# Audio tower on one Trainium2 core: the shared network's last product in eleven matmuls, and two reorderings beside it

## What is computed

```python
q, k, v = split(x, 3, axis=1)                       # each (128, 125, 512)
h = v @ softmax(q.T @ k / sqrt(125)).T              # per batch: 512 x 512 scores
n = layernorm(h)
h = h + attention(n; Wq, Wk, Wv, Wo)                # 8 heads, 2 kv heads, rope, tanh softcap 50
n = layernorm(h)
shared = (silu(n @ sw1) * (n @ sw3)) @ sw2          # sw2: 448 x 512
routed = top-2 of 8 experts (softmax(n @ gate_w) + bias), each the same network with w1, w3, w2
out = h + shared + routed
```

## Time and profile before

| | us |
|---|---|
| three runs | 6224.49, 6225.23, 6228.56 |
| median | 6225.23 |
| the profiled execution, device time | 6225.23 |
| its span, first to last instruction | 6223.5 |

### The profile page before, as it was taken

How to read it: one execution, slowest core, us unless ns; L and a number is a source line. 1 busy time by engine, 2 the same in 40 slices (tenths; PEclk the granted TensorE clock), 3 DMA queues, 4 the chain that set the end, 5 groups by cost and what they waited for, 6 DMA issues and landing times. The chain is left out here.

```text
span 6223.5 us, 108360 instructions
## 1 busy us (share of the span) xinstructions
PE 6034.7 (97%) x32968; PEld 5134.6 (83%) x32968; DVE 3931.3 (63%) x9812; ACT 2617.3 (42%) x4904; POOL 2608.1 (42%) x1865
## 2 busy tenths in 40 slices
PE   5999999999999999999999996999999999999999
PEld 4888888888888888888888885888888888888888
DVE  4777777777777777777777774444444444444444
ACT  3444444444444444444444442333333333333332
POOL 1333333333333333333333333555555655555554
PEclk8999999999999999999999998999999999999999
DMA  2111111111111111111111113555555555555541
GB/s 69 48 44 44 47 41 47 44 44 47 42 49 41 46 45 43 48 41 48 43 44 47 42 40 102 138 143 141 143 144 143 132 140 145 137 143 144 143 105 48
DMA packets 273407, 495.61 MB, mean 80 GB/s; under 512 B 39444, under 2 KB 112148, under 8 KB 273236
## 3 DMA queue, kind: packets, MB, share of 16 engines
q1 hardware_dynamic: 202452, 363.37, 19.6%
q0 software_dynamic: 70912, 131.71, 10.4%
HBM read 370.13 MB, written 140.28 MB: 82 GB/s over the span
## 5 line engine op out<-in xcount | busy, mean ns | idle before, releaser
L1325 POOL DMA_INDIRECT out_dram<-res,goal x280 | 519.4, 1855 | 929.9 <-DVE res L1261 446.1
L619 ACT ACTIVATE e<-ps,shift 128x512 f32<-128x512 f32 x512 | 347.9, 684 | 671.1 <-DVE shift L718 635.3
L1193 ACT ACTIVATE rT_hi<-ps 128x512 fp32r<-128x512 f32 x280 | 167.9, 600 | 1040.2 <-PE ps L1129 1040.2
L1119 PE MATMUL ps<-e_hi,rT_hi 128*128 128x448 f32 x2240 | 596.9, 388 | 5.2 <-ACT rT_hi L1193 5.2
L1303 POOL TENSOR_TENSOR e_lo<-raw,e_hi 128x1792 fp32r<-128x1792 f32 x140 | 568.6, 4062 | 9.8 <-ACT e_hi L1188 6.5
L1261 DVE COPY res<-ps 128x512 f32<-128x512 f32 x280 | 193.7, 692 | 594.8 <-PE ps L1119 579.8
L1119 PE MATMUL ps<-e_lo,rT_hi 128*128 128x448 f32 x2240 | 550.8, 367 | 0.0
L1119 PE MATMUL ps<-e_hi,rT_lo 128*128 128x448 f32 x2240 | 549.4, 367 | 0.0
L904 POOL TENSOR_SCALAR ve<-ag 125x1 f32<-125x1 f32 x256 | 57.1, 223 | 1124.7 <-DVE ag L734 1087.0
L1119 PEld LDWEIGHTS ps<-e_hi,rT_lo 128*128 128x128 f32 x2240 | 421.2, 188 | 37.8
L1119 PEld LDWEIGHTS ps<-e_lo,rT_hi 128*128 128x128 f32 x2240 | 421.2, 188 | 37.3
(11 more groups left out here) (203 smaller groups left out, 15377.0 us busy)
## 6 DMA issues: line engine op xcount, KB each, us to landing
raw<-in_L_ffn_w SPq DMA_DIRECT2D x210, 896.0 KB, 5.6
X<-in_x SPq DMA_DIRECT2D x128, 750.0 KB
normed_rows<-y SPq DMA_DIRECT2D x128, 250.0 KB
out_dram<-h SPq DMA_DIRECT2D x128, 250.0 KB
rows<-normed_rows,entries POOLq DMA_INDIRECT x280, 4.8
out_dram<-res,goal POOLq DMA_INDIRECT x280
routed_entries<-entry,slot POOLq DMA_INDIRECT x256
raw<-in_L_ffn_sw SPq DMA_DIRECT2D x3, 896.0 KB
```

What stands on the lines that cost most here:

```text
L619: nc.scalar.activation(e[:, i, :], ps[:, (i + 1) % 2, :], ACT.Exp, scale=QS, bias=shift[:, i:i + 1], accum_out=total[:, i:i + 1]).then_inc ...
L1119: ins = nc.tensor.matmul(dst, lhs[a][:rows_, k, :], rhs[b][:rows_, k, 0:width], start=(k == 0 and i == 0), stop=(k == KC - 1 and i == 2))
L1325: nc.gpsimd.indirect_dma_start(out, bass.IndirectOffsetOnAxis(ap=goal[group[1] % 2][:, i:i + 1], axis=0), res[i % 2][:], None, bounds_chec ...
```

## The change

`sw2` has 448 = 3 x 128 + 64 rows. It is now held as three pieces 128 deep and a fourth whose lower and upper 64 partitions both hold the last 64 rows (two loads into `raw_2[:, 3, :]`). The hidden activation is cut alike (`turn_inner`: three transposes of 128 columns and one of 64). Of its last piece the high part stands in partitions 0 to 63 of `hT[0]`, and the low part, which was in `hT[1]`, in partitions 64 to 127 of the same. One matmul with `w2s` high then does high x high and low x high at once; the other, with `w2s` low (zero in the upper half), does high x low. So three pieces take three matmuls each and the last takes two: 11.

Since `down_part(3, 0)` now needs the low part too, the downs are put elsewhere: four ahead of `scores(2)` (two ahead of the X transposes, two behind, the second of these waits for `hT_lo`), none between `scores(2)` and `scores(3)`, four behind the xn transposes. Three stay at the step's end. ScalarE makes hT_hi, and VectorE the low part, in two instructions each.

On ScalarE xT_hi now comes ahead of vT_high. On GpSimd vT_low now comes behind the second `rstd` and the two scatters.

```diff
-        w2s = resident("w2s", [HW, HC, D])
+        w2s = resident("w2s", [P, HC, D])
+        TAIL = HID - 3 * P
...
-                    load(raw_2[:, :, :], sw2.rearrange("(k p) h -> p k h", p=HW))
+                    load(raw_2[:, 0:3, :], sw2[0:3 * P, :].rearrange("(k p) h -> p k h", p=P))
+                    for q in range(2):
+                        load(raw_2[q * TAIL:(q + 1) * TAIL, 3, :], sw2[3 * P:HID, :])
...
+                    nc.vector.memset(w2s[1][TAIL:P, 3, :].bitcast(F32), 0.0)
+                    nc.vector.tensor_tensor(w2s[1][:, 0:3, :], raw_2[:, 0:3, :], w2s[0][:, 0:3, :].bitcast(F32),
+                                            ALU.subtract)
+                    nc.vector.tensor_tensor(w2s[1][0:TAIL, 3, :], raw_2[0:TAIL, 3, :],
+                                            w2s[0][0:TAIL, 3, :].bitcast(F32), ALU.subtract).then_inc(s_lo, 1)
...
-                        return nc.tensor.matmul(ps[0:C, 6, :], hT[c][0:HW, k, 0:C], w2s[part][0:HW, k, 0:D],
+                        return nc.tensor.matmul(ps[0:C, 6, :], hT[c][:, k, 0:C], w2s[part][:, k, 0:D],
                                                 start=(k == 0 and part == 0 and c == 0), stop=last)
+
+                    def turn_inner():
+
+                        for k in range(3):
+                            nc.tensor.transpose(ps[:, 4, k * C:(k + 1) * C], gb[0:C, k * P:(k + 1) * P],
+                                                ident[0:C, 0:C])
+                        return nc.tensor.transpose(ps[0:TAIL, 4, 3 * C:4 * C], gb[0:C, 3 * P:HID], ident[0:C, 0:C])
...
                     if has(3):
-                        down_part(3, 0)
                         down_part(0, 1)
+                        down_part(1, 1)
...
                         last.then_inc(vT_ps.sem, 1)
+                    if has(3):
+                        down_part(2, 1)
+                        pe.wait_ge(hT_lo.sem, hT_lo.at(g))
+                        down_part(0, 0, c=1)
                     if has(0):
                         scores(2)
-                    if has(3):
-                        for k in range(1, HC):
-                            down_part(k, 1)
                     if has(0):
                         scores(3)
...
                     if has(3):
 
-                        pe.wait_ge(hT_lo.sem, hT_lo.at(g))
-                        for k in range(HC):
-                            last = down_part(k, 0, c=1, last=(k == HC - 1))
-                        last.then_inc(dn_ps.sem, 1)
+                        for k in (1, 2):
+                            down_part(k, 0, c=1)
+                        down_part(3, 0)
+                        down_part(3, 1, last=True).then_inc(dn_ps.sem, 1)
...
                         weights(2)
                         weights(3)
+                    if has(1):
+                        act.wait_ge(xT_ps.sem, xT_ps.at(a))
+                        act.wait_ge(kv_ps.sem, kv_ps.at(f))
+                        hi_part(xT, 3, P).then_inc(xT_hi.sem, 1)
+                    if has(0):
                         act.wait_ge(vT_sb.sem, vT_sb.at(t))
                         act.wait_ge(o_ps.sem, o_ps.at(a))
                         nc.scalar.activation(vT[0][:, :, :], vT_full[:, :, :], ACT.Copy).then_inc(vT_hi.sem, 1)
...
-                        hi_part(hT, 4, HW).then_inc(hT_hi.sem, 1)
+                        nc.scalar.activation(hT[0][:, 0:3, 0:C], ps[:, 4, 0:3 * C].rearrange("p (k c) -> p k c", k=3),
+                                             ACT.Copy)
+                        nc.scalar.activation(hT[0][0:TAIL, 3, 0:C], ps[0:TAIL, 4, 3 * C:4 * C],
+                                             ACT.Copy).then_inc(hT_hi.sem, 1)
...
-                        lo_part(hT, 4, HW).then_inc(hT_lo.sem, 1)
+                        nc.vector.tensor_tensor(hT[1][:, 0:3, 0:C],
+                                                ps[:, 4, 0:3 * C].rearrange("p (k c) -> p k c", k=3),
+                                                hT[0][:, 0:3, 0:C].bitcast(F32), ALU.subtract)
+                        nc.vector.tensor_tensor(hT[0][TAIL:P, 3, 0:C], ps[0:TAIL, 4, 3 * C:4 * C],
+                                                hT[0][0:TAIL, 3, 0:C].bitcast(F32),
+                                                ALU.subtract).then_inc(hT_lo.sem, 1)
```

More of the change, by code:

```diff
@@ L126, in audio_tower @@
         w3s = resident("w3s", [P, KC, HID])
-        w2s = resident("w2s", [HW, HC, D])
+        w2s = resident("w2s", [P, HC, D])
+        TAIL = HID - 3 * P
+        assert 2 * TAIL == P and HC == 4
         cos_t = sbuf("cos_t", [P, HD], F32, tower)
@@ L154, in audio_tower @@
             raw_3 = sbuf("raw_3", [P, KC, HID], F32, c0)
-            raw_2 = sbuf("raw_2", [HW, HC, D], F32, c0)
+            raw_2 = sbuf("raw_2", [P, HC, D], F32, c0)
             trif = sbuf("trif", [P, P], F32, c0)
@@ L158, in audio_tower @@
             n_loads = [0]
-            N_LOADS = NH + 11
+            N_LOADS = NH + 13
             jobs = [(raw_q[:, j, :], wqkv, P * j) for j in range(KC)]
@@ L226, in _ @@
                         dve.wait_ge(s_hi, len(jobs) + n + 1)
-                        nc.vector.tensor_tensor(w[1][:], raw[:], w[0][:].bitcast(F32), ALU.subtract).then_inc(s_lo, 1)
+                        if n < 2:
+                            nc.vector.tensor_tensor(w[1][:], raw[:], w[0][:].bitcast(F32), ALU.subtract).then_inc(s_lo, 1)
+                    nc.vector.memset(w2s[1][TAIL:P, 3, :].bitcast(F32), 0.0)
[3 more added lines that the diff above has]
+                                            w2s[0][0:TAIL, 3, :].bitcast(F32), ALU.subtract).then_inc(s_lo, 1)
                 @block.tensor
@@ L554, in step @@
                         pe.wait_ge(rope_sb.sem, rope_sb.at(a))
-                        turn(4, HW, gb).then_inc(hT_ps.sem, 1)
+                        turn_inner().then_inc(hT_ps.sem, 1)
                     if has(1):
@@ L640, in step @@
                         weights(3)
-                        act.wait_ge(vT_sb.sem, vT_sb.at(t))
-                        act.wait_ge(o_ps.sem, o_ps.at(a))
-                        nc.scalar.activation(vT[0][:, :, :], vT_full[:, :, :], ACT.Copy).then_inc(vT_hi.sem, 1)
                     if has(1):
@@ L647, in step @@
                         hi_part(xT, 3, P).then_inc(xT_hi.sem, 1)
+                    if has(0):
+                        act.wait_ge(vT_sb.sem, vT_sb.at(t))
+                        act.wait_ge(o_ps.sem, o_ps.at(a))
+                        nc.scalar.activation(vT[0][:, :, :], vT_full[:, :, :], ACT.Copy).then_inc(vT_hi.sem, 1)
                     if has(2):
@@ L925, in step @@
                         rstd(a, ag1, ve1, rs1, ag1_sb, ve1_sb, rs1_sb, xn_sb)
-                    if has(0):
-                        pool.wait_ge(vT_hi.sem, vT_hi.at(t))
-                        pool.wait_ge(o_ps.sem, o_ps.at(a))
-                        alone(pool)
-                        nc.gpsimd.tensor_tensor(out=vT[1][:, :, 0:C], in0=vT_full[:, :, :],
-                                                in1=vT[0][:, :, 0:C].bitcast(F32),
-                                                op=ALU.subtract).then_inc(vT_lo.sem, 1)
                     if has(2):
@@ L944, in step @@
                                 oob_is_err=False).then_inc(scattered.of(g), 16)
+                    if has(0):
+                        pool.wait_ge(vT_hi.sem, vT_hi.at(t))
+                        pool.wait_ge(o_ps.sem, o_ps.at(a))
+                        alone(pool)
+                        nc.gpsimd.tensor_tensor(out=vT[1][:, :, 0:C], in0=vT_full[:, :, :],
+                                                in1=vT[0][:, :, 0:C].bitcast(F32),
+                                                op=ALU.subtract).then_inc(vT_lo.sem, 1)
                     if has(1):
```

## The result

| | before | after |
|---|---|---|
| median of four runs, us | 6224.86 (6222.73 to 6228.56) | 6144.91 (6143.91 to 6147.20) |
| span of the profiled execution, us | 6223.5 | 6142.1 |
| mean granted TensorE clock | 0.991 | 0.991 |

The kernel became 80 us faster: ratio 0.9871, interval 0.9854 to 0.9889. 6143 was predicted.

What follows compares the result with a forecast made beforehand. TensorE's instruction stream plus its few waits was taken to bound the tower. 0.61 + 0.04 = 0.65 us a step over 125 steps gives 81.3, with start and end terms 82: 6225.2 to 6143 us, 8-in-10 range 6129 to 6180.

Steps and rivals of the forecast that it cites:

- The bound: Tower: TensorE's instruction stream plus its waits sets the step of about 28.7 us; largest wait 0.7 us, ahead of scores(2).
- The fourth rival: Ahead of scores(2): the hole travels with the downs, only 0.275 gained, 6191 us; chance 0.16 together with the second rival.
- Scores(3) charged with 0.09: Scores(3), directly behind scores(2), pays 0.09 us for a first matmul and no wait; wo begins 0.60 earlier.
- q's release, taken as 0.05 behind xT_hi's end: With the swap xT_hi ends at 1012.54, so q may begin at 1012.59, ahead of its slot 1012.65; gain held 0.61.
- the second rival: Exponentials' chain takes back the filled hole at scores(2), scores(3) or q: 6191 to 6175 us; chance 0.16 with the fourth.
- One matmul fewer: 0.235 a step: Down product: 11 matmuls instead of 12, depth 128 changing nothing in the slot, saves 0.235 us a step.
- vT_low as the cause of the odd steps' stop: GpSimd's vT_low delays the chain to e's transposes, 0.08 every second step; moving it gains 0.04 a step on average.
- The GpSimd move as needed beside the swap: With vT_high later, vT_low (1.29 us) would push GpSimd's second rstd by up to a microsecond; behind the scatters it doesn't.
- The swap: ScalarE makes xT_hi ahead of vT_high; without this the 0.60 gained ahead of q would shrink to about 0.1.
- The 64-wide transpose at 0: Fourth gb transpose, 64 columns, taken to cost nothing; bounds 0 and 0.17 to 0.34 us for array shape changes.
- hT in two instructions, hidden: hT split on ScalarE and VectorE: +0.06 us on VectorE, about the same on ScalarE; VectorE's 0.43 us standing hides its part.
- Small terms: Outside the full steps: start +1 us (bounds 0 to 5), first two q steps gain 1.1, three drain steps 0.7.

Runs made afterwards that it cites:

- e3_reorders: Kernel before with the two reorderings alone (xT_hi ahead of vT_high, vT_low behind the scatters), its 12 matmuls where they were: 6221.82 us, ratio 0.9993.
- e12_merge_wait: Merged matmul at the old places, both reorderings, with TensorE's wait for place moved ahead of the xn transposes: 6194.02 us against 6192.93 without that move.
- e10_maxima: Changed kernel with VectorE's maxima of scores(2) and (3) moved ahead of xn, nothing else: 6141.61 us, ratio 0.9862 to the kernel before.
- e9_both: Changed kernel with two VectorE moves: maxima ahead of xn, reciprocal and first quarter of e's scaling ahead of y: 6125.21 us, ratio 0.9836 to the kernel before.
- e1_act_old: Changed kernel with the ScalarE swap undone, vT_high again ahead of xT_hi: 6204.97 us, ratio 0.9964 to the kernel before.
- e7_wide: Changed kernel with gb padded by 64 zero columns, so its fourth transpose has 128 columns: 6143.63 us, ratio 0.9866 to the kernel before.
- e5_fill_only: Kernel before, 12 matmuls 112 deep, with both reorderings and four downs ahead of scores(2), five behind xn's transposes; no merge: 6146.94 us, ratio 0.9871.
- e14_merge_five: Merged matmul at the old places, both reorderings, but one down moved from between the scores to behind xn's transposes, five there: 6177.29 us, ratio 0.9924.
- e11_fill_moves: New placement without the merge (12 matmuls, five downs behind xn's transposes) plus both VectorE moves (maxima, scaling of e): 6140.64 us, ratio 0.9865.
- e6_merge_only: Changed kernel, 11 matmuls and both reorderings, with the downs placed as before the change: 6192.93 us, ratio 0.9946 to the kernel before.

## Why the prediction was right, and where it wasn't

The total (6143 against 6144.9) and the 0.65 us a step (0.650) held. The parts of the sum held less well: errors of about 0.1 us a step cancelled, so that the total came within 2 us is in part luck.

- **The bound.** Right. TensorE's stream with its waits is the step. The wait ahead of scores(2), 0.7 us in the earlier trace rows, fell to 0.45 by the printed idle time, with 0.19 of empty slot, and scores(2) stayed 1.08 behind X: the exponential sets it. The fourth rival is out.
- **Scores(3) charged with 0.09.** Wrong: it cost nothing. Its weights load at 1016.50, 0.14 ahead of the slot. So wo came 0.69 earlier, not 0.60.
- **q's release, taken as 0.05 behind xT_hi's end, and so just ahead of the slot.** Wrong by 0.08. It is 0.13 in after and 0.12 in e3_reorders. The start-up step in the earlier trace rows is one of those written out one by one, where it is 0.05 in every kernel, and didn't stand for those of the loop; the pair of the running step (xT_hi's end at 1013.11, q's weights at 1013.24) was at hand. With the slot at 0.70 instead of 0.60 this made q 0.11 late. Net at q: 0.59, where 0.61 was forecast. This is the mechanism of the second rival, at a third of its price. e12_merge_wait shows that 0.07 of the 0.12 goes with the wait for `place`. That this wait asks for nothing in the start-up step is not the reason for the 0.05: steps 3 to 5 and 126 to 128 have it too, and there it asks for something.
- **"One matmul fewer: 0.235 a step."** The term that failed, though the sum didn't show it. It holds at the old places (29 us), but beside the filled hole it is 0.02 to 0.03, since the downs behind xn are also the cover of xT_hi, and a slot taken out of a cover that is just long enough is given back as waiting. Had I asked of each down what it hides, I would have put most of the gain on the placement.
- **vT_low as the cause of the odd steps' stop.** Wrong. With GpSimd idle the rstd still begins 0.22 to 0.28 behind the aggregate's end, and e3_reorders keeps the stop. After the change the distance in the odd step is 0.50 and not 0.56, but its weights still load only as the transposes begin, and the first eight then take 0.85 (1026.37 to 1027.22) where in the other steps, with weights 0.11 ahead, they take 0.79:

```profile
1026.37 0.86 PEld L461 LDWEIGHTS ps<-ident,e 128*128 128x128 f32 x8
...
1026.37 1.09 PE L461 MATMUL ps<-ident,e 128*128 128x128 f32 x8
1027.22 1.07 PE L355 MATMUL ps<-w1g_hi,yT_hi 128*125 128x456 f32 x4
```

  So the stop went from 0.08 to 0.02 us, and was not gone, as I had expected. The cause is the scaling of e on VectorE, which is just too late when q is on time: e10_maxima puts q on time and brings the stop back, e9_both moves the scaling and it is gone. The gain of 0.04 a step was there (y to e 1.90 to 1.86), for another reason: q's own 0.11 of delay gives the scaling room. Another 0.03 came behind e, which I didn't forecast. Half of it lies in those first eight transposes (0.82 in the mean, 0.835 before); the rest is open.
- **The GpSimd move as needed beside the swap.** Right. Up to a microsecond was said for the second rstd, and it begins 0.95 later against its input. What that does to the step was given no price: 0.93, 116 us in all, more than the whole gain.
- **The swap.** Right: "without the swap the 0.60 would shrink to about 0.1" stands against 0.65 less 0.47 (e1_act_old), about 0.2.
- **The 64-wide transpose at 0.** Right, shown by e7_wide.
- **hT in two instructions, hidden.** Nothing in the step shows it.
- **Small terms.** The start was taken as +1 us and was -0.3: the first scores begin at 59.64 instead of 59.91. VectorE's last pieces grew from 2.29 to 2.92 us (0.48, 1.76, 0.68), 0.63 where I had taken 0.4, but ended earlier than before (46.88 for 47.27), so nothing waited for them. The drain was taken as -0.7 and was 0: the marks of steps 127 and 129 are as far apart as before. The first steps, taken as -1.1, were +0.6. Together they came out 1.1 us against the forecast.

## What to carry to other kernels

An instruction in a full stream has two values: the slot that it takes, and the latency of another engine that it covers. Before taking one out, or moving it into a hole, list what each one hides; and measure two edits together and apart, since here 29 and 75 us made 77, not 104. When several edges are all within 0.1 us, removing one gains little (3 and 5 us) and removing all gains the sum and more (20).

## What the runs showed of the hardware that I had not expected

- **Late weights have a price of their own, and it is graded.** When q's first weights load 0.01 or 0.02 us ahead of the first matmul, the first four matmuls take 1.02 to 1.03 us (after, e3_reorders); at 0.08 ahead 0.95 or 0.96 (e12_merge_wait); at 0.12 to 0.23 ahead 0.93 to 0.95 (e5_fill_only, e14_merge_five, e11_fill_moves). The first eight transposes of e show the same: 0.85 us with weights that load as they begin, 0.81 at 0.045 ahead (e3_reorders, e6_merge_only, every second step), 0.79 at 0.11. Scores(3), with its weights 0.14 ahead, costs nothing.
- **A second wait behind the one that matters costs 0.06 to 0.07 us in the steps of the loop**, though what it asks for has long been there: from ScalarE's end to the weights 0.05 to 0.06 with one wait (e12_merge_wait), 0.12 to 0.13 with two. In the steps written out one by one it costs nothing: 0.05 with two waits as well. Why is open.
- **From VectorE's aggregate to GpSimd's add** it is 0.22 to 0.28 us though GpSimd is idle for 5 us or more. An "issue" bracket there isn't a busy engine.
- **A fuller stream didn't lower the clock**: 1.00 granted with TensorE busy in 99.9% of the tower, by the profile's own measure.
